# A fused recurrent-memory and spiking layer: norm statistics finished by GpSimd instead of VectorE, and ScalarE's queue reordered

## The chip, the cores and the metric

The kernel runs on one core of a Trainium2 chip. The metric is device time in microseconds (us), the median of several executions; lower is better. TensorE (PE in the profile; its weight loads are PEld), VectorE (DVE), ScalarE (ACT), GpSimd (POOL) and SyncE (SP) are processors with a queue each. Each works through its queue strictly in the order written, and they meet only through semaphores.

## The reference

The input is `x`, 8 batches of 512 tokens by 256 features. The layer is

```python
x = x + layernorm(attention(layernorm(x)))
x = x + layernorm(ffn(layernorm(x)))
```

with `layernorm(x) = (x - mean) / sqrt(var + 1e-5)` over the 256 features. `attention` projects to q, k and v (16 heads of 16), normalizes k inside each head, and runs a recurrence over the 512 tokens, `F = retention * F + coef * outer(v, k)`, `y = (W_LTM + F) q`, followed by an output projection. `ffn` is `relu(x W_fc)^2 W_proj`, followed by five spiking steps whose number of spikes, over 5, is its output. So every batch has four norms: norm 1 (input of attention), norm 2 (its output), norm 3 (input of the feed-forward part), norm 4 (the spike counts).

## The kernel before, in words

Everything is fp32 in on-chip memory. A batch is four tiles of 128 tokens (`TILES` = 4), or, with features first, two tiles of 128 features by 512 tokens.

**Slots.** The code is a software pipeline over batches. Function `run` calls `iteration(g, ...)` for g = 0 to 9 on every engine, and each iteration has 16 slots s. In iteration g the recurrence of batch g runs (flag `now`), while batch g+1 is prepared (`after`, b = g+1: norm 1, transposes, projections of k, q, v), batch g-1 goes through the output projection, norms 2 and 3 and the first feed-forward matmul (`before`, b1), and batch g-2 through the second feed-forward matmul, the spikes and norm 4 (`two_before`, b2). Iterations 2 to 6 have all four parts. Iteration 7 has no `after`, iteration 8 only `before` and `two_before`, iteration 9 only `two_before`. The slot and the place inside a slot fix the order of every engine's queue by hand; nothing else plans it.

**The recurrence.** In each slot VectorE makes two products (`hebbian`, L722) and two scans over 512 tokens (`scan`, L732). GpSimd multiplies the two states by q (`read`, L873, one 128x1024 operation per slot, done one slot later), and TensorE adds the products up every second slot (`sums`, L324). `read(g, 15)` stands in slot 0 of the next iteration, and `sums(g, 7)` in its slot 1. Reading needs the scans (`state_done`) and a free buffer of four (`sum_done`); the scans need a read buffer of four (`prod_done`).

**A norm.** VectorE's `statistics` makes `bn_stats` over four tiles (L679) and joins them with four `bn_aggr` (L686) into mean and variance. ScalarE's `deviation` takes the square root (L462). VectorE's `scales` takes the reciprocal (L692). ScalarE scales the four tiles (`norm`, L468; `norm4`, L474). Norms 1 to 3 subtract no mean (their inputs are centred through the weights); norm 4 does, through the offsets `nmr` = -mean/deviation, four small VectorE operations in `spike_offsets` (L697). GpSimd adds norm 4's result to the residual (`add_feed_forward`, L884, slot 13), and SyncE stores it.

**The keys.** `square_k` on ScalarE, `key_variance` on TensorE (L301), `key_deviation` on ScalarE (L497), `key_reciprocal` on VectorE (L709, `krd`), `spread_k`, `key_scale` on TensorE (L310), `norm_k` on VectorE (L714), and `copy_key` on ScalarE into PSUM (`p_k`), which the products read. This runs twice per batch: for half 1 in slots 1 to 8, for half 0 of the next batch in slots 11 to 16.

**The turn and the spikes.** In slots 6 and 7 TensorE transposes the normed input of the next batch into the bank `p_a` (`turn_x`, L275), and ScalarE copies each half out twice (`copy_xt`, L479: `xf`, then `xt`). The four parts of the second feed-forward matmul (`down`, L346) are copied by `copy_yf` (`yf`), five `signs` per pair of tiles follow (L547), and TensorE adds them up (`count_spikes`, L354). The count of the second pair waits for `signs(b2, 1)` in slot 8.

**ScalarE's queue before**, where the change touches it. Slot 0: `copy_key`, `deviation(1)`, `copy_v`, `hidden` 6 and 7. Slot 2: `copy_y`, `key_deviation`, `norm1`. Slot 3: two `copy_o`, `copy_q`. Slot 6: `copy_xt(b, 0)`, `copy_yf(b2, 2)`. Slot 7: `deviation(3)`. Slot 8: `copy_key`, `copy_xt(b, 1)`, `copy_yf(b2, 3)`, `norm` 3, `signs(b2, 1)`. Slot 11: `copy_y`, `deviation(4)`, `square_k`, `hidden` 1 and 2. Slot 12: `key_deviation`, `norm4`. Slot 13: `copy_q`, `spread_k`, `hidden` 3 and 4. Slot 15: `hidden` 5. A `hidden` is a Relu (L535, frees the bank for the up projection after next, L371) and a Square (L537).

Of the kernel before, what the change touches and what calls it, by code (L numbers as in the profile page):

```python
# [16 lines left out]
P = 128  # L17
# [51 lines left out]
def build(nc, x, w_qkv, w_o, w_fc, w_proj, w_ltm, head_params, shared_params, ident, head_mask, pick, out):  # L69
    ctx = ExitStack()  # L70
    with ctx:
# [6 lines left out]
        def sem(name):  # L78
# [34 lines left out]
        nmr = sb("nmr", [P, TILES])  # L113

# [42 lines left out]
            ones_ready wv_mean wv_centred wkq_mean wkq_centred wide_mean wide_copied wide_centred wo_mean wo_centred tables_done setup_step  # L157
# [6 lines left out]
            sign_done count_done spk_done n4_stats n4_var n4_dev n4_step n4_done res_done""".split()}  # L164
# [284 lines left out]
        def _(act):  # L449
# [9 lines left out]
            def deviation(n, b):  # L459
                act.wait_ge(S[f"n{n}_var"], at(b + 1))  # L460
                eps = eps_sb[:, 1:2] if n == 4 else eps_sb[:, 0:1]
                nc.scalar.activation(dev[n - 1][:, :], moments[n - 1][:, :, 1], ACT.Sqrt, bias=eps).then_inc(S[f"n{n}_dev"], 1)  # L462
# [8 lines left out]
            def norm4(b):  # L471
                act.wait_ge(S["n4_step"], at(2 * (b + 1)))
                for u in range(TILES):
                    nc.scalar.activation(spk[:, u, :], spk[:, u, :], ACT.Identity, scale=rdev[3][:, u:u + 1],  # L474
                                         bias=nmr[:, u:u + 1]).then_inc(S["n4_done"], 1)
# [110 lines left out]
            def iteration(g, now, before, two_before, after):  # L586
                b, b1, b2 = g + 1, g - 1, g - 2
                for s in range(SLOTS):
# [6 lines left out]
                    if s == 0:  # L595
                        if now and before: copy_key(g, 0)
                        if after: deviation(1, b)
                        if now: copy_v(g, 1)
                        if two_before:
                            hidden(b2, 6)  # L600
                            hidden(b2, 7)
                    if s == 1:
                        if now: square_k(g, 1)
                    if s == 2:
                        if before: copy_y(b1, 1)
                        if now: key_deviation(g, 1)
                        if after: norm1(b)
                    if s == 3:
                        if before:
                            copy_o(b1, 0)  # L610
                            copy_o(b1, 1)
                        if now: copy_q(g, 1)
                    if s == 4:
                        if before: deviation(2, b1)
                        if now: spread_k(g, 1)
                        if two_before: copy_yf(b2, 0)
# [49 lines left out]
        def _(dve):  # L666
# [8 lines left out]
            def statistics(n, b, src, ready, count):  # L675
# [6 lines left out]

                dve.wait_ge(S[f"n{n}_stats"], at(b + 1))
                dve.wait_ge(S[f"n{n}_step"], at(b if n < 4 else 2 * b))
# [52 lines left out]
            for j in range(STEPS):  # L737
                v.memset(drive_sb[:, j:j + 1], -DRIVES[j])
            v.memset(ones_sb[:, :], 1.0 / D).then_inc(S["ones_ready"], 1)
# [94 lines left out]
            def iteration(g, now, before, two_before, after):  # L834
                b, b1, b2 = g + 1, g - 1, g - 2
                for s in range(SLOTS):
# [10 lines left out]
                    if after and s == 2: scales(1, b)  # L847
                    if now and s == 4: key_reciprocal(g, 1)
                    if before and s == 4: statistics(2, b1, oo, "o_done", 2 * (b1 + 1))
                    if before and s == 5: scales(2, b1)  # L850
                    if now and s == 6: norm_k(g, 1)
                    if before and s == 7: statistics(3, b1, x1[b1 % 2], "x1_done", b1 + 1)
# [12 lines left out]
        def _(pool):  # L865
# [30 lines left out]

            low_x(0, 0)
# [13 lines left out]
            def iteration(g, now, before, two_before, after):  # L911
                b, b1, b2 = g + 1, g - 1, g - 2
                for s in range(SLOTS):
                    if s > 0 and now: read(g, s - 1)
# [8 lines left out]
                    if two_before and s == 13: add_feed_forward(b2)  # L923
# [53 lines left out]
```

## Time and profile before

| | |
|---|---|
| median of 3 runs | 638.61 us (637.57 to 639.96) |
| the profiled execution's own time | 633.62 us |
| its span, first to last instruction | 631.8 us |
| busy: VectorE / TensorE / GpSimd / ScalarE | 534.2 / 497.6 / 389.0 / 328.7 us |
| mean granted TensorE clock | 0.886 of full speed |

The span and the profiled execution's own time belong together; 1.8 us lie around the span. The median of the runs is 5.0 us above that execution. The first 35 us are setup, the recurrence runs from 35 us to 549 us, and the rest, some 83 us, finishes the last two batches without it. A busy share is an average over these stages. Which engine sets the pace in one of them has to be read from who waits for whom there.

### The profile page before, as it was taken

Reading aid. Unit: us, or ns where it says so; the run is one execution under the profiler, and the core shown is the slowest. Engines: PE = TensorE matmul, PEld = TensorE weight load, DVE = VectorE, ACT = ScalarE, POOL = GpSimd, SP = SyncE. Lnnn points to the kernel's source line nnn. Section 1 sums busy time; section 2 is a strip of 40 time slices with the busy share of each in tenths; the row PEclk is TensorE's granted clock in tenths of the full one; section 3 lists DMA queues with packets and bytes.
Section 4 is the critical chain, followed back from the end, with each engine's and each line's share of the span. In section 5 each row is a group of like instructions: output and inputs, shape, how many; then the busy total and the mean of one; then the engine's idle time right before and its main releaser. Section 6 shows DMA issues by size and latency. Waiting matters only on the chain.

```text
span 631.8 us, 7778 instructions
## 1 busy us (share of the span) xinstructions
PE 497.6 (79%) x2264; PEld 325.4 (52%) x2272; DVE 534.2 (85%) x933; ACT 328.7 (52%) x641; POOL 389.0 (62%) x186
## 2 busy tenths in 40 slices
PE   3585548359996999699969997899879996896891
PEld 1341225136673667365736575566646664484670
DVE  4799999997999999999999998999999999712001
ACT  4532113245647754675466636654666455636634
POOL 0048975785567766877687756875787677710201
PEclk9877667659997999899989989799979997978896
DMA  7475566456644774466556653577347844200000
GB/s 238 112 210 144 162 154 186 131 143 160 182 133 116 188 209 137 133 167 200 149 149 152 176 170 107 147 182 206 100 117 202 215 101 133 67 1 0 33 1 33
DMA packets 54730, 87.63 MB, mean 139 GB/s; under 512 B 5409, under 2 KB 19361, under 8 KB 54689
## 3 DMA queue, kind: packets, MB, share of 16 engines
q1 hardware_dynamic: 54112, 87.12, 49.9%
q8 instruction: 18, 0.29, 0.2%
q14 instruction: 24, 0.19, 0.1%
q10 hardware_dynamic: 576, 0.03, 0.1%
HBM read 78.74 MB, written 8.39 MB: 138 GB/s over the span
## 4 chain that ended last, share of the span: by engine, by line
PE 51%; issue 16%; DVE 15%; ACT 10%; POOL 6%; DMA 1%; POOLq 0%; ACTq 0%; DVEq 0%
PE p_c L346 13%; PE p_c L371 12%; DVE state L732 9%; PE p_a L281 6%; PE p_y L324 5%; PE p_c L337 4%; POOL prod L873 3%; ACT sign L547 3%; PE p_c L354 2%; PE p_a L301 2%; POOL x1t L889 2%; DVE p_u L722 2%; PE p_y L319 2%; ACT oo L468 1%; PE p_c L363 1%
## 5 line engine op out<-in xcount | busy, mean ns | idle before, releaser
L873 POOL TENSOR_TENSOR prod<-state,qf 128x1024 f32<-128x1024 f32 x128 | 303.1, 2373 | 140.4 <-DVE state L732 121.9
L732 DVE TENSOR_TENSOR_SCAN state<-ret,p_u 128x512 f32<-128x512 f32 x256 | 309.2, 1209 | 0.0
L722 DVE TENSOR_TENSOR p_u<-vrep,p_k 128x512 f32<-128x512 f32 x256 | 171.5, 676 | 2.5 <-ACT p_k L479 2.5
L346 PE MATMUL p_c<-wproj_sb,ht 128*128 128x256 f32 x512 | 116.1, 382 | 1.3 <-ACT ht L537 1.3
L346 PEld LDWEIGHTS p_c<-wproj_sb,ht 128*128 128x128 f32 x512 | 95.7, 190 | 24.3 <-issue 9.2
L371 PE MATMUL p_c<-x1t,wfc_s 128*128 128x512 f32 x384 | 98.9, 410 | 9.1 <-POOL x1t L889 8.0
L281 PE MATMUL p_a<-xt,wqkv_s 128*128 128x512 f32 x276 | 82.7, 438 | 10.6 <-POOL xt L889 3.0
L371 PEld LDWEIGHTS p_c<-x1t,wfc_s 128*128 128x128 f32 x384 | 73.9, 196 | 31.3 <-POOL x1t L889 12.3
L324 PE MATMUL p_y<-prod,summer 128*32 128x512 f32 x512 | 76.8, 675 | 10.4 <-POOL prod L873 10.4
L281 PEld LDWEIGHTS p_a<-xt,wqkv_s 128*128 128x128 f32 x276 | 53.3, 203 | 45.7 <-issue 16.9
L535 ACT ACTIVATE hr<-p_c 128x512 f32<-128x512 f32 x64 | 38.2, 597 | 34.6 <-PE p_c L371 32.6
L354 PE MATMUL p_c<-sign,ident_b 128*128 128x512 bf16 x72 | 24.2, 476 | 35.6 <-ACT sign L547 34.6
L547 ACT ACTIVATE sign<-yf,drive_sb 128x512 bf16<-128x512 f32 x80 | 50.6, 709 | 0.3
L679 DVE BATCH_NORM_STATS2 stats<-spk 128x6 f32<-128x256 f32 x32 | 11.1, 408 | 41.1 <-ACT spk L479 41.1
L884 POOL TENSOR_TENSOR x<-x,spk 128x1024 f32<-128x1024 f32 x8 | 19.2, 2398 | 42.2 <-ACT spk L474 42.2
L537 ACT ACTIVATE ht<-hr 128x512 f32<-128x512 f32 x64 | 40.4, 632 | 2.0
L462 ACT ACTIVATE dev<-moments,eps_sb 128x4 f32<-128x4 f32 x32 | 9.5, 297 | 53.5 <-DVE moments L686 53.5
L889 POOL TENSOR_TENSOR xt<-xf,xt 128x512 fp32r<-128x512 f32 x16 | 20.4, 1276 | 24.9 <-ACT xt L479 24.9
L337 PE MATMUL p_c<-wo_sb,yt 128*128 128x256 f32 x128 | 34.1, 426 | 0.8 <-ACT yt L479 0.8
L354 PEld LDWEIGHTS p_c<-sign,ident_b 128*128 128x128 bf16 x80 | 7.6, 109 | 51.8 <-ACT sign L547 38.5
L324 PEld LDWEIGHTS p_y<-prod,summer 128*32 128x32 f32 x512 | 10.6, 114 | 41.2 <-issue 24.1
L889 POOL TENSOR_TENSOR x1t<-x1f,x1t 128x512 fp32r<-128x512 f32 x16 | 20.1, 1280 | 17.5 <-ACT x1t L479 17.5
(107 smaller groups left out, 505.2 us busy)
## 6 DMA issues: line engine op xcount, KB each, us to landing
vrep<-v_rows SPq DMA_DIRECT2D x256, 256.0 KB, 3.6
xa<-in_x SPq DMA_DIRECT2D x8, 512.0 KB, 5.3
v_rows<-vf SPq DMA_DIRECT2D x16, 256.0 KB, 2.3
x<-in_x SPq DMA_DIRECT2D x8, 512.0 KB, 4.5
out<-x SPq DMA_DIRECT2D x8, 512.0 KB, 3.3
ht<-in_w_fc SPq DMA_DIRECT2D x1, 1024.0 KB, 7.6
wproj_sb<-in_w_proj SPq DMA_DIRECT2D x1, 1024.0 KB, 10.1
state<-in_w_qkv SPq DMA_DIRECT2D x1, 512.0 KB, 5.8
```

Source lines behind the costliest of these rows:

```text
L281: last = pe.matmul(bank[:, :], wqkv_s[:, i, t, first_col:first_col + P], xt[:, j, t, :], start=(t == i == j == 0), stop=(t == KT - 1 and i ...
L324: last = pe.matmul(p_y[32 * grp:32 * grp + 32, :], summer[:, half, dl, grp, :], prod[:, s % NZ, grp % 2, :], start=False, stop=(dl == 3), ...
L337: last = pe.matmul(p_c[(t + 1) % 2][:, i * D:(i + 1) * D], yt[:, half, tokens(2 * t + i)], wo_sb[:, half, :], start=(half == 0), stop=(hal ...
L346: last = pe.matmul(p_c[(u + 1) % 2][:, 0:D], ht[:, f, tokens(u)], wproj_sb[:, f, :], start=(f == 0), stop=(f == FT - 1))
L354: last = pe.matmul(p_c[(pair + 1) % 2][:, :], ident_b[:, :], sign[:, pair, j, :, :], start=(j == 0), stop=(j == STEPS - 1))
L371: last = pe.matmul(p_c[(f + 1) % 2][:, :], wfc_s[:, i, t, f * P:(f + 1) * P], x1t[:, j, t, :], start=(t == i == j == 0), stop=(t == KT - 1 ...
L537: nc.scalar.activation(ht[:, f, :], hr[:, f % 2, :], ACT.Square).then_inc(S["h_done"], 1)
L547: last = nc.scalar.activation(sign[:, pair, j, :, :], yf[:, 2 * pair:2 * pair + 2, :], ACT.Sign, bias=drive_sb[:, j:j + 1], scale=BELOW_ONE)
L722: v.tensor_tensor(p_u[n % NU][:, :], vrep[:, n % NV, :], p_k[:, :], ALU.mult).then_inc(S["hebb_done"], 1)
L732: v.tensor_tensor_scan(state[:, s % NS, i, :], ret[:, r:r + 1].broadcast_to([P, L]), p_u[n % NU][:, :], 0.0, ALU.mult, ALU.add).then_inc(S ...
L873: p.tensor_tensor(prod[:, s % NZ, :, :], state[:, s % NS, :, :], qf[:, s // HS, :].unsqueeze(1).broadcast_to([P, 2, L]), ALU.mult).then_in ...
L889: p.tensor_tensor(low, value, high.bitcast(F32), ALU.subtract).then_inc(S[done], 1)
```

## The change

- `statistics` on VectorE now only makes `bn_stats`. For norms 2 and 3 the `bn_aggr` follow as before (now `moments_of`). For norms 1 and 4 GpSimd joins the statistics: each `bn_stats` of 256 values leaves count, mean and sum of squares for its even and for its odd values, and GpSimd forms the sum of squares of all 256 as the sum of both plus (8 x difference of means)^2. These are five 128x4 `tensor_tensor` operations for norm 1 and six for norm 4 (it also needs the sum of the means), three of them followed by a wait for their own completion (`step`). ScalarE's square root takes `scale=1/D` with them.
- The spike offsets move from four VectorE operations to two GpSimd ones, with a `step` between.
- ScalarE's order: `deviation(1)` from slot 0 to slot 2, ahead of `copy_y`; `norm1` from slot 2 to the end of slot 3; `copy_xt(b, 0)` from slot 6 to slot 7, behind `deviation(3)`; `deviation(4)` behind `square_k` in slot 11; `norm4` from slot 12 to slot 14, behind `hidden` 3 and 4.
- VectorE: `scales(1)` from slot 2 to 3, `scales(4)` from slot 12 to 13, ahead of `key_reciprocal`.
- GpSimd: `moments_of(1)` at the head of slot 1, `moments_of(4)` at the head of slot 11, `spike_offsets` at the head of slot 14, `add_feed_forward` from slot 13 to slot 15, where it stands ahead of `read(g, 15)`.
- Two constant tiles are set on VectorE at the start. GpSimd waits for them, then makes `moments_of(1, 0)`.

```diff
@@ scalar @@
             def deviation(n, b):
                 act.wait_ge(S[f"n{n}_var"], at(b + 1))
-                eps = eps_sb[:, 1:2] if n == 4 else eps_sb[:, 0:1]
-                nc.scalar.activation(dev[n - 1][:, :], moments[n - 1][:, :, 1], ACT.Sqrt, bias=eps).then_inc(S[f"n{n}_dev"], 1)
+                if n in (1, 4):
+                    eps = eps_sb[:, 1:2] if n == 4 else eps_sb[:, 0:1]
+                    nc.scalar.activation(dev[n - 1][:, :], squares[n][:, :], ACT.Sqrt, bias=eps, scale=1.0 / D).then_inc(
+                        S[f"n{n}_dev"], 1)
...
             def norm4(b):
-                act.wait_ge(S["n4_step"], at(2 * (b + 1)))
+                act.wait_ge(S["n4_offset"], at(b + 1))
...
                     if s == 0:
                         if now and before: copy_key(g, 0)
-                        if after: deviation(1, b)
...
                     if s == 2:
+                        if after: deviation(1, b)
                         if before: copy_y(b1, 1)
                         if now: key_deviation(g, 1)
-                        if after: norm1(b)
                     if s == 3:
...
                         if now: copy_q(g, 1)
+                        if after: norm1(b)
...
                     if s == 6:
-                        if after: copy_xt(b, 0)
                         if two_before: copy_yf(b2, 2)
                     if s == 7:
                         if before: deviation(3, b1)
+                        if after: copy_xt(b, 0)
...
                         if now: copy_y(g, 0)
+                        if after: square_k(b, 0)
                         if two_before: deviation(4, b2)
-                        if after: square_k(b, 0)
...
                         if after: key_deviation(b, 0)
-                        if two_before: norm4(b2)
...
+                    if s == 14 and two_before: norm4(b2)
@@ vector @@
-            def spike_offsets(b):
-                dve.wait_ge(S["n4_step"], at(2 * b + 1))
-                for u in range(TILES):
-                    last = v.tensor_scalar(nmr[:, u:u + 1], moments[3][:, u, 0:1], rdev[3][:, u:u + 1], -1.0, ALU.mult,
-                                           ALU.mult)
-                last.then_inc(S["n4_step"], 1)
...
-                    if two_before and s == 12:
-                        scales(4, b2)
-                        spike_offsets(b2)
+                    if two_before and s == 13: scales(4, b2)
@@ gpsimd @@
+            def moments_of(n, b):
+                pool.wait_ge(S[f"n{n}_stats"], at(b + 1))
+                pool.wait_ge(S[f"n{n}_dev"], at(b))
+                means = [stats[n - 1][:, :, i] for i in (1, 4)]
+                sums = [stats[n - 1][:, :, i] for i in (2, 5)]
+                if n == 4:
+                    p.tensor_tensor(twice_mean[:, :], means[0], means[1], ALU.add)
+                p.tensor_tensor(squares[n][:, :], sums[0], sums[1], ALU.add)
+                step(p.tensor_tensor(spread[n][:, :], means[0], means[1], ALU.subtract))
+                step(p.tensor_tensor(spread[n][:, :], spread[n][:, :], eight[:, :], ALU.mult))
+                step(p.tensor_tensor(spread[n][:, :], spread[n][:, :], spread[n][:, :], ALU.mult))
+                p.tensor_tensor(squares[n][:, :], squares[n][:, :], spread[n][:, :], ALU.add).then_inc(S[f"n{n}_var"], 1)
+
+            def spike_offsets(b):
+                pool.wait_ge(S["n4_step"], at(b + 1))
+                pool.wait_ge(S["n4_done"], at(TILES * b))
+                step(p.tensor_tensor(twice_mean[:, :], twice_mean[:, :], minus_half[:, :], ALU.mult))
+                p.tensor_tensor(nmr[:, :], twice_mean[:, :], rdev[3][:, :], ALU.mult).then_inc(S["n4_offset"], 1)
...
                 for s in range(SLOTS):
+                    if after and s == 1: moments_of(1, b)
+                    if two_before and s == 11: moments_of(4, b2)
+                    if two_before and s == 14: spike_offsets(b2)
                     if s > 0 and now: read(g, s - 1)
...
-                    if two_before and s == 13: add_feed_forward(b2)
+                    if two_before and s == 15: add_feed_forward(b2)
```

## Rows read from the trace of the kernel before

**Rows 1.** The page's first part: busy us (share of the span) x instructions.

```profile
PE 497.6 (79%) x2264; PEld 325.4 (52%) x2272; DVE 534.2 (85%) x933; ACT 328.7 (52%) x641; POOL 389.0 (62%) x186
```

**Rows 2.** Timeline of VectorE: start us, us, engine, line, operation [idle before <-releaser].

```profile
276.55 0.58 DVE L697 TENSOR_SCALAR nmr<-moments,rdev 128x1 f32<-128x1 f32 x4
...
280.81 0.35 DVE L709 RECIPROCAL krd<-kdev 128x32 f32<-128x32 f32 x1 [0.25 <-ACT kdev L497]
...
289.62 1.38 DVE L679 BATCH_NORM_STATS2 stats<-xa 128x6 f32<-128x256 f32 x4
291.03 0.38 DVE L686 BATCH_NORM_AGGREGATE moments<-stats 128x2 f32<-128x6 f32 x4
...
321.61 0.38 DVE L686 BATCH_NORM_AGGREGATE moments<-stats 128x2 f32<-128x6 f32 x4
...
354.89 1.38 DVE L679 BATCH_NORM_STATS2 stats<-xa 128x6 f32<-128x256 f32 x4
...
421.82 1.38 DVE L679 BATCH_NORM_STATS2 stats<-xa 128x6 f32<-128x256 f32 x4
```

**Rows 3.** Who waited for whom: us in total, times, longest us.

```profile
PE p_y L324 <- POOL prod L873: 10.4, 4, 4.7
DVE krd L709 <- ACT kdev L497: 4.7, 6, 3.4
```

**Rows 4.** The chain that ended last, 288 to 352 us, its shares by line.

```profile
by line: PE p_c L346 22.2%; PE p_c L371 15.8%; PE p_a L281 9.4%; PE p_y L324 7.8%; PE p_c L337 5.6%; issue 5.3%; ACT sign L547 4.8%; POOL x1t L889 3.8%; PE p_c L354 3.6%; PE p_a L301 3.2%; PE p_y L319 2.7%; ACT oo L468 2.1%; ACT hr L535 1.9
```

**Rows 5.** Timeline of ScalarE in iterations 3 and 4.

```profile
288.25 0.60 ACT L535 ACTIVATE hr<-p_c 128x512 f32<-128x512 f32 x1 [1.71 <-PE p_c L371]
...
321.59 0.59 ACT L479 COPY xf<-p_a 128x512 f32<-128x512 f32 x1 [3.54 <-PE p_a L275]
...
322.73 0.37 ACT L479 COPY yf<-p_c 128x256 f32<-128x256 f32 x1
323.00 0.30 ACT L462 ACTIVATE dev<-moments,eps_sb 128x4 f32<-128x4 f32 x1
...
329.79 0.56 ACT L479 COPY spk<-p_c 128x512 f32<-128x512 f32 x1
```

**Rows 6.** Timeline of TensorE in iterations 4 and 7.

```profile
293.48 1.06 PE L324 MATMUL p_y<-prod,summer 128*32 128x512 f32 x8
...
297.56 1.06 PE L301 MATMUL p_a<-mean_sb,ksq 128*128 128x8 f32 x8 [1.44 <-ACT ksq L493]
...
329.94 2.31 PE L354 MATMUL p_c<-sign,ident_b 128*128 128x512 bf16 x5 [4.86 <-ACT sign L547]
...
524.25 1.46 PE L354 MATMUL p_c<-sign,ident_b 128*128 128x512 bf16 x5 [3.54 <-ACT sign L547]
```

**Rows 7.** Window: busy of PE, PEld, DVE, ACT, POOL; granted clock; DMA; GB/s.

```profile
330.00:332.00 2.00, 2.00 (x5) 0.74 (x6) 2.00 (x4) 0.35 (x1) 2.00 (x3) 0.50 0.94 243
```

**Rows 8.** GpSimd: timeline, then groups (busy, mean ns | idle before).

```profile
0.24 0.10 POOL L966 MEMSET const-float32-0.0<- 128x1 f32 x1 [0.24 <-issue]
...
285.19 7.11 POOL L873 TENSOR_TENSOR prod<-state,qf 128x1024 f32<-128x1024 f32 x3
...
L873 POOL TENSOR_TENSOR prod<-state,qf 128x1024 f32<-128x1024 f32 x128 | 303.1, 2373 | 140.4 <-DVE state L732 121.9 <-PE p_y L324 18.5
L889 POOL TENSOR_TENSOR x1t<-x1f,x1t 128x512 fp32r<-128x512 f32 x16 | 20.1, 1280 | 17.5 <-ACT x1t L479 17.5
```

**Rows 9.** Timelines of ScalarE, GpSimd and TensorE in the setup and the tail.

```profile
9.03 0.30 ACT L462 ACTIVATE dev<-moments,eps_sb 128x4 f32<-128x4 f32 x1 [0.20 <-DVE moments L686]
...
544.51 7.06 POOL L873 TENSOR_TENSOR prod<-state,qf 128x1024 f32<-128x1024 f32 x3
...
551.63 1.16 PE L324 MATMUL p_y<-prod,summer 128*32 128x512 f32 x8 [2.73 <-POOL prod L873]
...
595.50 4.37 PE L371 MATMUL p_c<-x1t,wfc_s 128*128 128x512 f32 x18 [1.15 <-ACT hr L535]
...
623.98 2.07 ACT L474 ACTIVATE spk<-spk,nmr,rdev 128x256 f32<-128x256 f32 x4 [0.86 <-DVE nmr L697]
```

More of the change, by code:

```diff
@@ L113, in build @@
         nmr = sb("nmr", [P, TILES])
+        squares = {n: sb(f"squares{n}", [P, TILES]) for n in (1, 4)}
+        spread = {n: sb(f"spread{n}", [P, TILES]) for n in (1, 4)}
+        twice_mean = sb("twice_mean", [P, TILES])
+        eight = sb("eight", [P, TILES])
+        minus_half = sb("minus_half", [P, TILES])
         xa = sb("xa", [P, TILES, D])
@@ L156, in build @@
             setup_ready setup_exp centred wv_high wv_low wk_high wk_low wq_high wq_low wide_high wide_low
-            ones_ready wv_mean wv_centred wkq_mean wkq_centred wide_mean wide_copied wide_centred wo_mean wo_centred tables_done setup_step
+            halves_set ones_ready wv_mean wv_centred wkq_mean wkq_centred wide_mean wide_copied wide_centred wo_mean wo_centred tables_done setup_step
             n1_stats n1_var n1_dev n1_step n1_done  xt_turned xt_done xt_high xt_low
@@ L163, in build @@
             up_done relu_done h_done down_done yf_done
-            sign_done count_done spk_done n4_stats n4_var n4_dev n4_step n4_done res_done""".split()}
+            sign_done count_done spk_done n4_stats n4_var n4_dev n4_step n4_offset n4_done pool_step res_done""".split()}
         v_in = [sem(f"v_in{i}") for i in range(NV)]
@@ L460, in deviation @@
                 act.wait_ge(S[f"n{n}_var"], at(b + 1))
-                eps = eps_sb[:, 1:2] if n == 4 else eps_sb[:, 0:1]
-                nc.scalar.activation(dev[n - 1][:, :], moments[n - 1][:, :, 1], ACT.Sqrt, bias=eps).then_inc(S[f"n{n}_dev"], 1)
+                if n in (1, 4):
+                    eps = eps_sb[:, 1:2] if n == 4 else eps_sb[:, 0:1]
+                    nc.scalar.activation(dev[n - 1][:, :], squares[n][:, :], ACT.Sqrt, bias=eps, scale=1.0 / D).then_inc(
+                        S[f"n{n}_dev"], 1)
+                else:
+                    nc.scalar.activation(dev[n - 1][:, :], moments[n - 1][:, :, 1], ACT.Sqrt, bias=eps_sb[:, 0:1]).then_inc(
+                        S[f"n{n}_dev"], 1)
             def norm(n, b, src, dst, used, count):
@@ L680, in statistics @@
                 last.then_inc(S[f"n{n}_stats"], 1)
+            def moments_of(n, b):
                 dve.wait_ge(S[f"n{n}_stats"], at(b + 1))
-                dve.wait_ge(S[f"n{n}_step"], at(b if n < 4 else 2 * b))
+                dve.wait_ge(S[f"n{n}_step"], at(b))
                 for u in range(TILES):
@@ L738, in _ @@
                 v.memset(drive_sb[:, j:j + 1], -DRIVES[j])
+            v.memset(eight[:, :], 8.0)
+            v.memset(minus_half[:, :], -0.5).then_inc(S["halves_set"], 1)
             v.memset(ones_sb[:, :], 1.0 / D).then_inc(S["ones_ready"], 1)
@@ L846, in iteration @@
                         scan(g, s, 0)
-                    if after and s == 2: scales(1, b)
+                    if after and s == 3: scales(1, b)
                     if now and s == 4: key_reciprocal(g, 1)
-                    if before and s == 4: statistics(2, b1, oo, "o_done", 2 * (b1 + 1))
+                    if before and s == 4:
+                        statistics(2, b1, oo, "o_done", 2 * (b1 + 1))
+                        moments_of(2, b1)
                     if before and s == 5: scales(2, b1)
                     if now and s == 6: norm_k(g, 1)
-                    if before and s == 7: statistics(3, b1, x1[b1 % 2], "x1_done", b1 + 1)
+                    if before and s == 7:
+                        statistics(3, b1, x1[b1 % 2], "x1_done", b1 + 1)
+                        moments_of(3, b1)
                     if two_before and s == 10: statistics(4, b2, spk, "spk_done", 2 * (b2 + 1))
-                    if two_before and s == 12:
-                        scales(4, b2)
-                        spike_offsets(b2)
+                    if two_before and s == 13: scales(4, b2)
                     if g == 0 and s == 13: mean_out()
@@ L895, in low_x1, with step, moments_of @@
                 rest(x1f[:, t, :], x1t[:, 0, t, :], x1t[:, 1, t, :], "x1t_high", KT * b + t + 1, "x1t_low")
+            steps = [0]
+            def step(ins):
+                steps[0] += 1
+                ins.then_inc(S["pool_step"], 1)
+                pool.wait_ge(S["pool_step"], steps[0])
+            def moments_of(n, b):
+                pool.wait_ge(S[f"n{n}_stats"], at(b + 1))
[14 more added lines that the diff above has]
+                p.tensor_tensor(nmr[:, :], twice_mean[:, :], rdev[3][:, :], ALU.mult).then_inc(S["n4_offset"], 1)
+            pool.wait_ge(S["halves_set"], 1)
+            moments_of(1, 0)
             low_x(0, 0)
```

## The prediction

> **What bounds the kernel now.** The page's busy shares come first and mislead: VectorE leads with 534.2 us [rows 1]. The timeline of VectorE gives the period: statistics of norm 1 start at 289.62, 354.89 and 421.82, so iteration 4 takes 65.27 us and iteration 5, 66.93 [rows 2]. VectorE fills nearly all of that, which looks like a bound. The waits say otherwise. VectorE stops for ScalarE's `kdev` (0.25 us at 280.81 [rows 2]; 6 times in all, one of 3.44 included [rows 3]), and that deviation follows TensorE's key variance. In the other direction TensorE's sums waited for GpSimd's products only 4 times [rows 3], in the first two iterations and the tail. The chain of waits through iteration 4 agrees: its thirteen largest entries are TensorE's, ScalarE's, issue time and one GpSimd operation that follows ScalarE; none is VectorE's [rows 4]. So in iterations 2 to 6 TensorE and ScalarE form a loop that paces itself, and VectorE has about 0.9 us spare in it. Iterations 0, 1 and 7 are paced by VectorE, setup and tail by the latency of a serial chain.
>
> The loop's one long hole is TensorE's wait of 4.86 us for the second pair of signs [rows 6]. Before them ScalarE works without a break from 321.59 (`xf`, released by TensorE) to 329.79 [rows 5], and TensorE then works at half clock until 334 us (0.50 in the window at 330 us [rows 7]).
>
> **The change part by part.** All terms are against the profiled execution's 633.62 us (span 631.8 and 1.8 around it). I carry the sum to the median, 5.0 us above, unchanged.
>
> *VectorE's removed work.* Four `bn_aggr` take 0.38 us and end as the next operation starts, about 0.40 from the queue [rows 2]. This goes twice per iteration. The offsets take 0.58, net 0.5 because the next operation overlaps [rows 2]. Together 1.3 us per full iteration. In iterations 2 to 6 it only lengthens the wait for `kdev`: worth 0 there, except for the phase below. In iterations 0 and 1 the queue is VectorE-bound up to that wait, and each loses one aggregate: **-0.8 us**.
>
> *GpSimd's price.* No small `tensor_tensor` is in the trace. A 128x1024 one costs 2373 ns, a 128x512 one 1280 [rows 8]. The line through both leaves 0.19 us at zero width. The ends are 0.10 (a one-column memset) and 1.28 (128x512) [rows 8]. I take 0.19, since four columns lie nearest to zero, and 0.25 for one followed by a step. `moments_of(1)` is then about 1.1 us, `moments_of(4)` 1.3, the offsets 0.5. The Trainium skill's GPSIMD Engine Reference (section 4.1) advises VectorE for elementwise work because GpSimd is about twice slower with two inputs. By that rule the move would lose; the sum below charges it only where the chain is serial.
>
> *Square roots in front.* In the block from 321.59, `yf` 2 and `dev` 3 stand at 322.73 and 323.00 behind `xf` and `xt` [rows 5]. Both come earlier now: `yf` 2 falls into the idle 3.54 us, and `dev` 3 goes as soon as its variance is there, 321.61 + 0.38 = 321.99 [rows 2]. VectorE reaches it 0.40 sooner (one aggregate less since `kdev`), so 321.6. It takes 0.2 of the queue, and `xf` starts at 321.83, 0.24 late. The block behind is shorter by 0.27 (`yf`) and 0.20 (`dev`). The spike count comes 0.23 us sooner. Five iterations (2 to 6): **-1.15 us**. `deviation(1)` in front of `copy_y` delays it 0.2, beside the key variance that starts at 297.56 [rows 6] and ends 0.9 later: 0. The waits of `norm1` and `deviation(4)` are covered by `copy_q` and `square_k`: 0.
>
> *`norm4` behind `hidden` 4.* Its 2.07 us [rows 9] go mostly into the 1.71 that `hidden` 5 waits for TensorE [rows 5]. `hidden` 5 comes some 0.3 late, and the bank it frees is needed just then: 0 to 0.1, taken as 0. Behind it `copy_key` is about 0.25 late, covered by statistics of norm 1 on VectorE, except in iteration 7, which has none.
>
> *`add_feed_forward` ahead of `read(g, 15)`.* Before, three reads ran without a gap from 285.19 to 292.30 [rows 8], the last one ending 1.2 us ahead of its sums at 293.48 [rows 6]. Now the addition of 2.4 us stands before the last one, while the others start up to 2.3 us earlier. Read 14 waits for its scan and ends at 288.7, `norm4` ends at 288.6, the addition at 291.1 and read 15 at 293.47. That is just when the sums want it: 0.05, taken as 0 per iteration. In iteration 7 nothing covers it. Reads ran from 544.51 to 551.57, and TensorE waits 2.73 us for the last [rows 9]. The addition puts 1.9 in front; VectorE's savings there (aggregate and offsets, 0.9, less 0.25 of `copy_key`) return 0.65: **+1.25 us**.
>
> *Setup and tail.* At the start, statistics to `dev` (9.03 [rows 9]) took 0.44 us. With GpSimd between it is 1.2, and VectorE's queue stands behind it: **+0.8**. In iteration 8 `norm4` moves from before `hidden` 3, where TensorE lost 1.15 [rows 9], to before `hidden` 5, where the last three hiddens queue behind it: **+0.3**. In iteration 9 all is serial. Moments cost 0.9 more than aggregates; offsets cost 0.5 against the 0.6 up to `norm4` at 623.98 [rows 9]: **+0.8**.
>
> Sum: -0.8 - 1.15 + 1.25 + 0.8 + 0.3 + 0.8 = **+1.2 us**. So 634.8 for such an execution and **639.8** for the median. At 1.28 us per small operation the serial places (5, 6 and 2 of them) add some 13 us; at 0.10 they give back 1.5.
>
> **The rivals.** *Slower: GpSimd's queue becomes late.* The place is read 15 behind the addition in slots 15 and 0. From the moment that read 15 ends over 0.3 us later than worked out (small operations of 0.6 us or more, or a late `norm4`), TensorE's sums, the key projection behind them and the loop lose it one for one. At 0.8 us in each of five iterations plus 2 more in setup and tail: 1.2 + 4 + 2, thus 645.8. For it speaks that the margin is nil at 293.47; against it that ScalarE is busy with `hidden` 7 then, which hides some 0.3, and that read 14 is timed by its scan. Chance 0.2.
>
> *Faster: TensorE's clock stays up.* The hole shrinks from 4.86 to about 4.4 us. The granted clock fell behind it in each of these iterations; at half clock the work from 329.94 to 334 costs about 2 us more than at full. If half the five falls are spared or shortened, -5: 634.8. Iteration 5 has a second fall behind the 1.44 us wait for `ksq`, which costs 66.93 - 65.27 = 1.7 [rows 2], and a shift of phase may remove or multiply it. The Trainium skill's TensorE: Matmul & The Clock Gate (section on HAM oscillation) says that idle gaps re-throttle the array and shorter ones keep it warm. By that rule any shortening could pay; the trace has a fall even behind a hole of 3.54 us, in iteration 7 [rows 6], which speaks against it. Chance 0.08.
>
> *Faster: VectorE is the bound after all.* If the loop follows VectorE's queue, 1.3 us in each of iterations 2 to 6 return: 6.5 less, 633.3. The nearly full queue speaks for it, the `kdev` waits against. Chance 0.1.
>
> *The change does nothing on the path* (no gain of 0.23, small costs as worked out): 641. It lies inside the forecast's own case.
>
> **How the numbers follow.** The forecast's case has 0.62 and spans 636 to 643: the price of small operations from 0.10 to 0.5, and one clock fall more or less (1.7). A measurement of this kernel can tell about 0.5%, 3.2 us, from no change: that is 635.4 to 641.8. Faster: 0.08 + 0.1, of which some ends inside: 0.16. Slower: 0.2 and the upper end of the forecast: 0.24. Same: 0.60. The range for 8 in 10 reaches down to 634 and up to 645.5.
>
> **What would show it.** Right: `bn_aggr` of norms 1 and 4 gone, VectorE busy down by some 10 us, its waits for `kdev` grown to about 1 us; the loop's period near 65.0; `dev` 3 ahead of `xf` and the hole at the signs near 4.4; the last read some 1.2 us later against its batch; small GpSimd operations near 0.2 us. Wrong: sums waiting for products in iterations 2 to 6, `kdev` waits unchanged with a period near 64, or small operations of 0.6 us and more.

## The result and the profile after

The changed kernel takes 640.74 us (median of 20 runs, 637.3 to 643.13), the kernel before 637.81 us (median of 20 runs beside them). The ratio is **1.0051**, 95% interval 1.0032 to 1.007: slower by about 3.2 us (interval 2.0 to 4.5), where 1.2 was forecast. The ratios here and below are those on record; they need not equal the quotient of two medians (2.9 us here). A second set of runs gave 1.003 (1.0005 to 1.0055), which has the forecast 1.2 us inside.

The page's busy line of the changed kernel, to be held against [rows 1]:

```profile
PE 502.4 (79%) x2272; PEld 328.1 (51%) x2272; DVE 521.8 (82%) x839; ACT 328.2 (51%) x641; POOL 407.8 (64%) x290
```

VectorE is relieved of 12.4 us, and the kernel is slower. The timeline of VectorE of the changed kernel (start us, us, operation [idle before <-releaser]) shows where the relief went:

```profile
37.43 1.40 DVE L689 BATCH_NORM_STATS2 stats<-xa 128x6 f32<-128x256 f32 x4
...
284.52 0.35 DVE L712 RECIPROCAL krd<-kdev 128x32 f32<-128x32 f32 x1 [1.37 <-ACT kdev L507]
...
293.33 1.38 DVE L689 BATCH_NORM_STATS2 stats<-xa 128x6 f32<-128x256 f32 x4
...
358.45 1.38 DVE L689 BATCH_NORM_STATS2 stats<-xa 128x6 f32<-128x256 f32 x4
...
425.02 1.38 DVE L689 BATCH_NORM_STATS2 stats<-xa 128x6 f32<-128x256 f32 x4
```

It waits 1.37 us for the key deviation (the `krd` row) where it waited 0.25 [rows 2]. Iteration 4 takes 65.12 us instead of 65.27 (iterations 2 and 3: 65.10 and 65.09), and iteration 5, 66.57 instead of 66.93. The recurrence opens at 37.43 us, read from the statistics that VectorE makes in its first slot. In the trace of before the same statistics stood at 32.38.

ScalarE's timeline shows the block ahead of the second signs, to be held against [rows 5]: deviation 3 comes first, `yf` 2 has gone into the idle time ahead.

```profile
321.27 0.35 ACT L489 COPY yf<-p_c 128x256 f32<-128x256 f32 x1
325.34 0.30 ACT L471 ACTIVATE dev<-moments,eps_sb 128x4 f32<-128x4 f32 x1 [3.71 <-DVE moments L696]
325.54 0.57 ACT L489 COPY xf<-p_a 128x512 f32<-128x512 f32 x1
...
333.25 0.57 ACT L489 COPY spk<-p_c 128x512 f32<-128x512 f32 x1
```

TensorE's timeline shows the turn, the second spike count, and in the tail the wait for the last product [rows 6, 9]:

```profile
324.76 0.60 PE L280 MATMUL p_a<-ident_sb,xa 128*128 128x128 f32 x4
...
333.40 2.32 PE L359 MATMUL p_c<-sign,ident_b 128*128 128x512 bf16 x5 [4.38 <-ACT sign L557]
...
555.43 1.94 PE L329 MATMUL p_y<-prod,summer 128*32 128x512 f32 x8 [4.78 <-POOL prod L880]
```

The hole is 4.38 us (4.86 before), and turn to count is 8.64 us. Before it was 9.04, from the turn below to the count at 329.94 [rows 6]:

```profile
320.90 0.60 PE L275 MATMUL p_a<-ident_sb,xa 128*128 128x128 f32 x4
```

GpSimd's timeline has the small operations in the setup, read 15 behind the addition where iteration 3 goes over into 4, and the same in the tail:

```profile
9.07 0.20 POOL L920 TENSOR_TENSOR squares<-stats 128x4 f32<-128x4 f32 x1 [8.63 <-DVE stats L689]
9.23 0.20 POOL L921 TENSOR_TENSOR spread<-stats 128x4 f32<-128x4 f32 x1
9.51 0.20 POOL L922 TENSOR_TENSOR spread<-spread,eight 128x4 f32<-128x4 f32 x1
...
290.19 2.41 POOL L880 TENSOR_TENSOR prod<-state,qf 128x1024 f32<-128x1024 f32 x1 [1.12 <-PE p_y L329]
292.56 2.40 POOL L891 TENSOR_TENSOR x<-x,spk 128x1024 f32<-128x1024 f32 x1
294.92 2.39 POOL L880 TENSOR_TENSOR prod<-state,qf 128x1024 f32<-128x1024 f32 x1
...
550.73 2.35 POOL L891 TENSOR_TENSOR x<-x,spk 128x1024 f32<-128x1024 f32 x1
553.03 2.35 POOL L880 TENSOR_TENSOR prod<-state,qf 128x1024 f32<-128x1024 f32 x1
```

The two profiled executions differ by 637.4 - 631.8 = 5.6 us, the medians by 2.9. The profiled execution of before took 633.62 us, 4.2 below its kernel's median; that of the changed kernel took 639.36, 1.4 below. So some 2.8 us of the differences in the table below come from which executions were profiled:

| stretch | before | changed | difference |
|---|---|---|---|
| start to statistics of norm 1, batch 1 | 32.38 | 37.43 | +5.05 |
| to the same of batch 7 (six iterations) | 389.44 | 387.59 | -1.85 |
| to the last scan's end | 127.32 | 126.12 | -1.20 |
| to the statistics of norm 2 in iteration 8 | 11.68 | 13.99 | +2.31 |
| to the last norm's statistics | 60.15 | 60.52 | +0.37 |
| to the end | 10.83 | 11.75 | +0.92 |

The setup is the one stretch far from the forecast, so the experiments start with it.

### The profile page after: what moved, and what is told of

It is laid out like the page before. It is cut to its first block, busy times and chain, and to the rows that moved or that the text cites. A ratio compares the mean times of both kernels' runs of the same rounds, so it can differ in the third digit from the quotient of the medians.

```text
span 637.4 us, 7804 instructions
## 1 busy us (share of the span) xinstructions
PE 502.4 (79%) x2272; PEld 328.1 (51%) x2272; DVE 521.8 (82%) x839; ACT 328.2 (51%) x641; POOL 407.8 (64%) x290
## 4 chain that ended last, share of the span: by engine, by line
DVE 33%; PE 29%; issue 21%; ACT 10%; POOL 4%; DMA 1%; POOLq 0%; DVEq 0%; ACTq 0%
DVE state L735 20%; PE p_c L376 7%; PE p_c L351 7%; DVE p_u L725 6%; DVE stats L689 4%; ACT sign L557 3%; PE p_a L286 3%; PE p_y L329 3%; PE p_c L359 2%; POOL x1t L896 2%; PE p_c L342 2%; POOL prod L880 2%; PE p_a L306 1%; ACT oo L478 1%; PE p_c L368 1%
## 5 line engine op out<-in xcount | busy, mean ns | idle before, releaser
L286 PE MATMUL p_a<-xt,wqkv_s 128*128 128x512 f32 x276 | 85.0, 447 | 11.6 <-POOL xt L896 4.4
L376 PEld LDWEIGHTS p_c<-x1t,wfc_s 128*128 128x128 f32 x384 | 72.5, 193 | 33.3 <-POOL x1t L896 13.3
L329 PE MATMUL p_y<-prod,summer 128*32 128x512 f32 x512 | 74.9, 660 | 12.7 <-POOL prod L880 12.7
L359 PE MATMUL p_c<-sign,ident_b 128*128 128x512 bf16 x80 | 27.2, 485 | 32.3 <-ACT sign L557 32.3
L342 PE MATMUL p_c<-wo_sb,yt 128*128 128x256 f32 x128 | 36.3, 447 | 0.9 <-ACT yt L489 0.9
L489 ACT COPY vf<-p_a 128x512 f32<-128x512 f32 x15 | 8.8, 586 | 47.3 <-PE p_a L286 47.3
L342 PEld LDWEIGHTS p_c<-wo_sb,yt 128*128 128x128 f32 x128 | 28.5, 229 | 7.4 <-issue 2.6
```

Of the source, the lines that this page charges most:

```text
L286: last = pe.matmul(bank[:, :], wqkv_s[:, i, t, first_col:first_col + P], xt[:, j, t, :], start=(t == i == j == 0), stop=(t == KT - 1 and i ...
L329: last = pe.matmul(p_y[32 * grp:32 * grp + 32, :], summer[:, half, dl, grp, :], prod[:, s % NZ, grp % 2, :], start=False, stop=(dl == 3), ...
L342: last = pe.matmul(p_c[(t + 1) % 2][:, i * D:(i + 1) * D], yt[:, half, tokens(2 * t + i)], wo_sb[:, half, :], start=(half == 0), stop=(hal ...
L359: last = pe.matmul(p_c[(pair + 1) % 2][:, :], ident_b[:, :], sign[:, pair, j, :, :], start=(j == 0), stop=(j == STEPS - 1))
L376: last = pe.matmul(p_c[(f + 1) % 2][:, :], wfc_s[:, i, t, f * P:(f + 1) * P], x1t[:, j, t, :], start=(t == i == j == 0), stop=(t == KT - 1 ...
```

## The experiments

Medians below are of runs taken beside runs of the kernel before. The kernel before itself had 639.58, 638.55 and 636.76 us in the three sets, so ratios are to be compared inside a set. In every full iteration TensorE's granted clock falls once near the spike count; "quiet" means an iteration without an additional fall.

**The changed kernel again.** No edit.

> The changed kernel once more, as the partner of the runs beside it. My theory: slower than the kernel before by 1.2 us of serial work plus whatever the setup adds, so a ratio of 1.002 to 1.006; the period of iterations 2 to 4 is 65.10 us again. The question it serves: the changed kernel's one trace opens the recurrence 5.05 us later than the trace of before (37.43 against 32.38 us), of which only 0.9 is GpSimd's chain. If TensorE's half clock in the setup is a matter of the execution, this trace may show another opening, nearer 33.5 us; if it follows from the change, it shows 37 us again.

Measured: 640.45 us against 639.58, ratio 1.003 (1.0005 to 1.0055). The recurrence opened at 33.23 us in this trace, 4.2 us before the other one of the same kernel:

```profile
33.23 1.39 DVE L689 BATCH_NORM_STATS2 stats<-xa 128x6 f32<-128x256 f32 x4
```

That is 0.85 us behind the 32.38 of before, about GpSimd's chain: its square root starts 1.35 us after the statistics end (8.94 to 10.29 in the first trace), where it was 0.44. TensorE's timeline tells the two executions apart. The key projection of the setup, first in the trace of the result, then in this one:

```profile
25.73 2.93 PE L286 MATMUL p_a<-xt,wqkv_s 128*128 128x512 f32 x6 [1.07 <-DVE wqkv_s L805]
```

```profile
25.33 1.66 PE L286 MATMUL p_a<-xt,wqkv_s 128*128 128x512 f32 x6 [1.52 <-DVE wqkv_s L805]
```

The same six matmuls take 2.93 us at half clock and 1.66 at full. So most of the 5.05 us was the clock of one execution. Nor did it last. Here iterations 0, 1 and 2 took 61.09, 67.24 and 66.67 us where the first trace had 59.85, 65.85 and 65.10. At the start of iteration 3 the two executions stand at 228.23 and 228.24 us: nothing is left of the 4.2 us.

**Norm 1 of batch 0 on VectorE.**

```diff
-                if n in (1, 4):
+                if n in (1, 4) and not (n == 1 and isinstance(b, int) and b == 0):
...
             statistics(1, 0, xa, "x_in", 16)
+            moments_of(1, 0)
...
             pool.wait_ge(S["halves_set"], 1)
-            moments_of(1, 0)
```

> Norm 1 of batch 0 has its moments from VectorE's bn_aggr again, all else as changed. Theory A (the setup's loss is the 0.9 us of the serial GpSimd chain and the rest is chance of the clock): 0.9 us less than the changed kernel, reciprocal about 0.45 us after the deviation starts as before. Rival B (the late start pushes TensorE's setup work into the half clock each time): 3 to 5 us less than the changed kernel, and the recurrence opens near 32.5 us.

Measured: 639.82 us, ratio 1.0021 (0.9996 to 1.0045), 0.6 us under the changed kernel beside it, inside the noise. The opening was at 33.94 us. The size fits A and speaks against a loss of 3 to 5 us in each run, but it does not settle a smaller tendency. Over all thirteen traces of this study the seven with GpSimd in the setup opened at 33.2, 35.5, 37.0, 37.1, 37.2, 37.4 and 37.8 us (mean 36.5). The six without opened at 32.4, 33.6, 33.9, 34.5, 36.1 and 36.3 (mean 34.5). The means are 2.0 us apart, 0.9 of it the chain. The start follows the clock: the mean granted clock from 20 to 32 us is 0.68 to 0.86 in the six traces that open by 35.5 us, and 0.51 to 0.64 in the five later ones that have a record there. Whether GpSimd's chain makes the half clock more likely stays open. By the start of iteration 3 little of it is left. In the eleven traces with the changed order that start lies at 228.4 us on average with GpSimd in the setup (seven, 226.6 to 230.9) and at 227.7 without (four, 225.3 to 229.0).

**The addition of iteration 7 behind read 15.**

```diff
-                    if two_before and s == 15: add_feed_forward(b2)
+                    if two_before and s == 15 and g != B - 1: add_feed_forward(b2)
...
                     if s == 0 and before: read(b1, SLOTS - 1)
+                    if s == 0 and g == B: add_feed_forward(b2 - 1)
```

> Only in iteration 7 the feed-forward addition goes behind read 15 (in iteration 8's slot 0). Theory A (in the tail nothing covers the addition): read 15 starts 2.3 us earlier against the last scan, TensorE's wait for it falls from 4.78 to about 2.5 us, and the kernel takes 2.3 us less than the changed one. Rival B (the read is not what the tail waits for): no change.

Measured: 637.89 us, ratio 0.9984 (0.9957 to 1.001), 2.6 us under the changed kernel of the same set (640.45). TensorE's wait for read 15 falls from 4.78 to 2.96 us (2.5 expected):

```profile
552.20 1.93 PE L329 MATMUL p_y<-prod,summer 128*32 128x512 f32 x8 [2.96 <-POOL prod L880]
```

From the last scan to the statistics of norm 2 it is 11.41 us (13.99 and 13.54 in the two traces of the changed kernel). In this trace the next stretch took 62.05 us (60.52 and 60.65), so that 0.7 to 1.1 us of the gain reached the end; the 2.6 us are the medians', and the intervals of the two ratios overlap a little. Theory A holds: one queue position, in one of ten iterations, is the largest single loss of the change that a run shows.

**The last norm's moments and offsets on VectorE.** `moments_of(4, b2)` and four `tensor_scalar` stand in VectorE's slots 10 and 13 when b2 is the last batch, and GpSimd skips them then:

```diff
-                    if two_before and s == 13: scales(4, b2)
+                    if two_before and s == 10 and b2 == B - 1: moments_of(4, b2)
+                    if two_before and s == 13:
+                        scales(4, b2)
+                        if b2 == B - 1: spike_offsets(b2)
```

> The changed kernel with only the last batch's norm 4 (moments and offsets) on VectorE. Theory A: from the last statistics to the end 10.8 us as in the kernel before, not 11.75; 0.9 us less in all, which a measurement hardly tells. Rival B (the tail hides it): 11.75 us again.

Measured: 640.17 us, ratio 1.0042 (1.001 to 1.0075). The last stretch is 10.81 us (10.83 before, 11.75 changed): the 0.9 us are there in the trace, and the runs can't tell them, as expected.

**All serial places at once.** The three edits above, and `norm4` of batch 6 behind `hidden` 7:

```diff
-                    if s == 14 and two_before: norm4(b2)
+                    if s == 14 and two_before and g != B: norm4(b2)
...
                             hidden(b2, 7)
+                            if g == B + 1: norm4(b2 - 1)
```

> All serial places put right at once, the loop left as changed: batch 0's norm 1 and the last batch's norm 4 (moments and offsets) on VectorE, the addition of iteration 7 behind read 15, and norm4 of batch 6 behind hidden 7. Theory A: 0.9 + 2.3 + 1.0 + 1.1 = 5.3 us less than the changed kernel, about 2 us (0.3%) faster than the kernel before, a ratio near 0.997. Rival B (the loss sits in the steady iterations): ratio stays above 1.003.

Measured: 636.08 us against 639.58, ratio 0.9957 (0.9924 to 0.999). This beats the changed kernel of the same set by 4.4 us, near the 5.3 of theory A. The loss does not sit in the steady iterations. A second set tests its gain over the kernel before:

> The kernel with all serial places put right, once more with five rounds, to settle whether it beats both. It was 0.9957 of the kernel before, interval 0.9924 to 0.999. Theory A: the ratio stays between 0.993 and 0.999. Rival B (that was the luck of its rounds): 1.000 or more.

Measured: 635.18 us against 636.76, ratio 1.0003 (0.9976 to 1.0029). That is what rival B says: the gain over the kernel before did not repeat. The version no longer shows the change's loss in either set. In this one the kernel with only the last norm undone had 1.0042, and the one without the GpSimd part (below) 1.0043. That it beats the kernel before is not shown.

**Is VectorE the bound?** Idle work on it, twelve `bn_aggr` that nobody uses:

```diff
+                    if two_before and after and s == 12:
+                        for u in range(3 * TILES):
+                            v.bn_aggr(pad[:, u, :], stats[3][:, u % TILES, :])
                     if two_before and s == 13: scales(4, b2)
```

> The changed kernel with 12 idle bn_aggr (about 1.2 us) added on VectorE in slot 12 of iterations 2 to 6, whose result nobody uses. Theory A (TensorE and ScalarE pace these iterations, VectorE waits 1.37 us there for the key deviation): the wait shrinks to about 0.2 us and the period stays 65.1 us. Rival B (VectorE paces them): the period grows by 1.2 us, the time by 6 us.

Measured: 641.86 us, ratio 1.0059 (1.0027 to 1.0091). VectorE's timeline has the idle work, the wait, and the statistics that open iteration 4:

```profile
283.84 0.88 DVE L866 BATCH_NORM_AGGREGATE pad<-stats 128x2 f32<-128x6 f32 x12
...
288.65 0.35 DVE L713 RECIPROCAL krd<-kdev 128x32 f32<-128x32 f32 x1 [0.44 <-ACT kdev L508]
...
297.45 1.38 DVE L690 BATCH_NORM_STATS2 stats<-xa 128x6 f32<-128x256 f32 x4
```

The twelve took 0.88 us, not 1.2. The wait fell by about that, from 1.37 to 0.44 us, and iterations 4 and 5 took 64.93 and 65.36 us (iterations 2 and 3, with an additional clock fall each, 66.68 and 66.53). The rival asks for 0.9 us in each of five iterations. The ratio lies only 0.5 to 1.9 us above the changed kernel's two, and no quiet iteration grew by it: VectorE does not pace the changed kernel's steady iterations.

**GpSimd's margin.** One idle 128x512 operation ahead of read 15 in iterations 2 to 6:

```diff
+                    if s == 0 and before and two_before and after: p.tensor_tensor(pad[:, :], pad[:, :], pad[:, :], ALU.mult)
                     if s == 0 and before: read(b1, SLOTS - 1)
```

> The changed kernel with one idle 128x512 operation (1.28 us) on GpSimd ahead of read 15 in slot 0 of iterations 2 to 6. Theory A (read 15 ends exactly when TensorE's sums want it, and ScalarE's hidden 7 covers about 0.3 us more): TensorE's sums wait 1.2 us for the product and the period grows by 0.9 to 1.0 us, the time by 4 to 5 us. Rival B (GpSimd has room there): period unchanged.

Measured: 646.95 us (four runs), ratio 1.0134 (1.0083 to 1.0185), by the ratios 5.3 to 6.6 us above the changed kernel of the other sets, where 4 to 5 were expected. GpSimd's and TensorE's timelines:

```profile
362.82 1.05 POOL L959 TENSOR_TENSOR pad<-pad 128x512 f32<-128x512 f32 x1
...
366.26 1.06 PE L330 MATMUL p_y<-prod,summer 128*32 128x512 f32 x8 [0.96 <-POOL prod L882]
```

The idle operation took 1.05 us, the sums waited 0.96, and quiet iteration 4 took 65.81 us, 0.7 more (0.9 to 1.0 expected). Iterations 3 and 5 took 67.70 and 67.51 with an additional clock fall each; iteration 2, whose sums did not wait, kept 65.13. So the margin is about 0.1 us for TensorE's wait, and 0.25 more did not reach the period. The slow rival's mechanism is real. Small operations of 0.20 us just did not reach it.

**The swap alone, on the kernel before.**

```diff
                     if s == 6:
-                        if after: copy_xt(b, 0)
                         if two_before: copy_yf(b2, 2)
                     if s == 7:
                         if before: deviation(3, b1)
+                        if after: copy_xt(b, 0)
```

> The kernel before, with only the first half of the turned input's copies moved behind deviation 3. Theory A (the deviation takes its place only when VectorE delivers the variance, 0.4 us later here than in the changed kernel): the copy starts 0.64 us late, the block behind is 0.47 shorter, the period of iterations 2 to 4 grows from 65.27 to about 65.4 us; the time is the same within noise. Rival B (square roots in front are a gain by themselves): the period falls to 65.0 or less.

Measured: 636.65 us, ratio 0.9978 (0.9937 to 1.0019). The turn-to-count distance grew as theory A has it, 9.37 us against 9.04:

```profile
321.65 0.60 PE L275 MATMUL p_a<-ident_sb,xa 128*128 128x128 f32 x4
...
331.02 1.72 PE L354 MATMUL p_c<-sign,ident_b 128*128 128x512 bf16 x5 [4.41 <-ACT sign L547]
```

Iteration 2 took the expected 65.4 us (160.04 to 225.48). Yet iterations 3, 4 and 5 took 65.05, 65.06 and 65.06, less than in the kernel before. The windows around the count of iteration 4 (busy us (x) of PE, PEld, DVE, ACT, POOL, granted clock, DMA, GB/s) show why, first the kernel before, then this one:

```profile
328.00:330.00 2.00, 0.06 (x1) 0.07 (x2) 2.00 (x4) 2.00 (x5) 1.88 (x1) 0.50 0.95 279
...
334.00:336.00 2.00, 2.00 (x13) 0.94 (x13) 1.97 (x8) 1.54 (x3) 1.50 (x3) 1.00 0.00 0
```

```profile
328.00:330.00 2.00, 0.00 (x0) 0.00 (x0) 2.00 (x3) 2.00 (x4) 0.84 (x2) 1.00 0.98 246
330.00:332.00 2.00, 0.98 (x4) 0.46 (x5) 2.00 (x3) 1.43 (x3) 2.00 (x2) 0.92 1.09 329
332.00:334.00 2.00, 2.00 (x8) 1.35 (x7) 2.00 (x3) 0.90 (x2) 2.00 (x2) 0.50 0.44 102
334.00:336.00 2.00, 2.00 (x13) 0.65 (x12) 1.97 (x10) 1.94 (x4) 2.00 (x2) 0.73 0.00 0
```

Before, the clock fell in the hole and half clock lasted until 334 us, 4 us past the count at 329.94. Here it fell only after the count, near 332, and was back at 335, some 3.4 us of half clock on work. Iteration 2 of this same trace is the counter-check. There the clock was down before the count at 200.53, the half clock on work lasted 4.8 us, and the period was the expected 65.44:

```profile
200.00:202.00 2.00, 1.47 (x4) 0.58 (x5) 2.00 (x4) 0.94 (x2) 2.00 (x2) 0.50 1.09 300
```

So a distance 0.33 us longer was paid back where the fall was shorter. In these VectorE no longer waits for the key deviation at all (0.25 us before), only 0.91 us for a copied key: with the moments still on VectorE, its queue has no other wait left to give.

**The swap undone, on the changed kernel.** The reverse of the diff above.

> The changed kernel with only the turned input's first copies back in slot 6, ahead of deviation 3. Theory A (the block of ScalarE ahead of the second signs is 0.4 us shorter in the changed kernel, and the half clock behind it gives part of that back or takes it): the distance from TensorE's turn to the second spike count goes from 8.64 back to about 9.04 us, the hole from 4.38 to about 4.86. The period of a quiet iteration rises by 0.2 to 0.4 us if the half clock begins before the count as in the changed kernel, and less or not at all if it begins elsewhere. Time within 0.3% of the changed kernel. Rival B (the swap is worth nothing or a loss): distance and period unchanged.

Measured: 644.1 us (six runs), ratio 1.0123 (1.0089 to 1.0158). The changed kernel was not run in this set; its nearest relative there, with only the last norm's moments undone, has 640.17, 3.9 us or 0.6% less. The expected "within 0.3%" was missed. The hole is back at 4.85 us and turn to count at 9.04. Quiet iterations take 65.45 to 65.50 us, 0.38 more than in the changed kernel:

```profile
259.31 0.60 PE L280 MATMUL p_a<-ident_sb,xa 128*128 128x128 f32 x4
...
268.35 2.32 PE L359 MATMUL p_c<-sign,ident_b 128*128 128x512 bf16 x5 [4.85 <-ACT sign L557]
```

Rival B falls. Five such iterations are 1.9 us. In the one trace the rest came with clock falls (iteration 4 took 67.17 us, and 67.25 lie between the counts of iterations 5 and 6) and an opening at 37.84. Why all six runs are above 642.5 us stays open.

**The change without its GpSimd part.** The changed order, with `bn_aggr` and the offsets on VectorE for all four norms:

```diff
-                if n in (1, 4):
+                if False:
...
-                    if two_before and s == 13: scales(4, b2)
+                    if two_before and s == 13:
+                        scales(4, b2)
+                        spike_offsets(b2)
...
-                    if after and s == 1: moments_of(1, b)
-                    if two_before and s == 11: moments_of(4, b2)
-                    if two_before and s == 14: spike_offsets(b2)
```

> The changed kernel's order on all engines, with moments and offsets back on VectorE: the change without its GpSimd part. Theory A (VectorE's 1.3 us per iteration only lengthen its wait for the key deviation): quiet iterations take 65.0 to 65.2 us, as in the changed kernel, and VectorE's wait for the key deviation falls from 1.37 to about 0.1 us; the setup saves 0.9, the last norm 0.9, and the first two iterations and iteration 7 lose 1.7 together, so the time is that of the changed kernel within noise. Rival B (VectorE paces the loop): quiet iterations of 66 us or more, the time 5 us or more above the changed kernel.

Measured: 639.38 us, ratio 1.0043 (1.0016 to 1.007), between the changed kernel's 1.0051 and 1.003 of other sets, as A has it. The wait for the key deviation is 0.17 to 0.45 us. But quiet iterations take 65.49 to 65.52 us, not 65.1. ScalarE's and TensorE's timelines:

```profile
260.35 0.30 ACT L472 ACTIVATE dev<-moments,eps_sb 128x4 f32<-128x4 f32 x1 [3.72 <-DVE moments L697]
260.55 0.56 ACT L490 COPY xf<-p_a 128x512 f32<-128x512 f32 x1
```

```profile
259.36 0.60 PE L280 MATMUL p_a<-ident_sb,xa 128*128 128x128 f32 x4
...
268.41 2.31 PE L359 MATMUL p_c<-sign,ident_b 128*128 128x512 bf16 x5 [4.38 <-ACT sign L558]
```

The deviation starts 0.99 us after the turn, in the changed kernel 0.58 (325.34 - 324.76). In the changed kernel, with `bn_aggr` of norm 1 (0.40 us) gone from its queue, VectorE reaches the variance of norm 3 that much sooner, and ScalarE's block waits for it. Turn to count is 9.05 us against 8.64. So GpSimd's part is worth 0.4 us per steady iteration, by this one phase, and spends it again elsewhere: 0.9 us each in the setup and the last norm are shown.

## Why the prediction was right, and where it was off

- **The number** is nearer than the working. The median was forecast at 639.8 us and came at 640.74. The sum, though, was made for the profiled execution, 634.8 us, and the changed kernel's took 639.36. The 5.0 us from execution to median, carried unchanged, were 1.4 for the changed kernel and, over 20 runs, 4.2 for the kernel before, whose median came 0.8 below the 638.61 taken. That the two gaps met is in part luck. As a difference, 1.2 us were forecast, below the interval of the first set (2.0 to 4.5) and inside that of the second (0.3 to 3.5).
- **The bound** was read rightly. Relief of VectorE went into its wait (0.25 to 1.37 us), and 0.88 us of idle work went back into it without a trace in the quiet periods.
- **GpSimd's price** was right: 0.20 us measured, 0.28 from one stepped operation to the next, for 0.19 and 0.25 taken by the line through two wide operations. The fear that the move loses because GpSimd is slower (the Trainium skill, GPSIMD Engine Reference, section 4.1) was borne out only where the chain is serial.
- **Square roots in front**: turn to count fell by 0.40 us where I had 0.23, mostly because `xf` starts only 0.09 us later behind the turn (0.78 against 0.69), not 0.24. The period fell only by 0.17 (65.27 to 65.10). Followed along TensorE's timeline from the count of iteration 3, 0.23 us were given back: 0.09 in the work behind the count, 0.12 by the time of the sums at 294.74, around `hidden` 5 and the bank it frees, which I had put at 0, and 0.05 up to the sums that read 15 feeds, less 0.03 behind them. The sizes were off, not the mechanism.
- **Read 15**: the margin was seen. It ended at 297.31 us, 0.06 ahead of its sums at 297.37. The working was off in one point: read 14 waited for TensorE (1.12 us), not for its scan. In the tail the two traces have +2.31 and +1.86 us, where I had 1.9. The -1.20 us over iterations 6 and 7 can't be set against it: the second trace of the changed kernel took 128.24 us there, more than the 127.32 of before.
- **Iterations 0 and 1** were forecast 0.8 us shorter. Iteration 0 was 61.1 us in most traces of the changed order (61.53 before), the aggregate's 0.4. Iteration 1 is not paced by VectorE, as I had it: VectorE waits there 3.44 us for the key deviation before [rows 3], and 3.51 and 4.90 in the two traces of the changed kernel, with the clock. Its length ranges from 63.5 to 67.3 us over all traces.
- **Iteration 8** cost 0.37 (0.3 forecast) and **the last norm** 0.92 (0.8).
- **The setup term** treated TensorE's clock as unchanged. The serial part was 0.85 us for the 0.8 taken, but the opening moves by 5 us with the clock, from 32.4 to 37.8 us over thirteen traces.
- **The missing 2 us** (3.2 measured, 1.2 forecast) are not located. The setup is a poor place for them: of the 2.0 us between the groups' openings, 0.7 is left by iteration 3. The serial places together are worth 4.4 us by the medians, where the terms behind them had 3.8, and the steady gain was 0.06 us per iteration short. The rest lies within what clock falls move from one execution to the next.
- **The rivals**: GpSimd late is real as a mechanism, shown by the added operation, but did not decide. The fast clock rival did not come: holes of 4.38 us had a fall behind or in them each time, so "any shortening could pay" did not hold. The swap alone shows that a fall can be shortened by timing. VectorE as the bound was excluded for the changed kernel.

## What to carry to other kernels

A queue with 98% busy time (VectorE before: 64.19 of the 65.27 us of iteration 4) can still be off the path: look for its waits on the others, and for theirs on it, before paying for its relief. When work goes to an engine with slack, price three places apart: the steady loop, the serial setup, and the tail, where a queue position that was free in the loop (an addition ahead of the last read) costs most of its length (1.9 to 2.3 of 2.35 us). Undo such a move only where the chain is serial. And before stages of two traces are compared, hold each profiled execution against its kernel's median: here one lay 4.2 us below it and the other 1.4, which is as much as the effect.

## What was not expected of the hardware

- The granted clock in the windows is 1.00 from 8 to 40 us in the changed kernel, although the matmuls of that stretch show the half clock (2.93 us for six against 1.66). Where the record has no entry yet, the matmul's duration is the better witness.

```profile
24.00:32.00 8.00, 5.76 (x17) 3.99 (x16) 5.79 (x26) 3.45 (x7) 0.00 (x0) 1.00 0.41 121
```

- A fall of TensorE's clock is not placed by the wait alone. In iteration 4, behind holes of 4.86 (before), 4.38 (changed) and 4.41 us (swap alone), work at half clock lasted 4.1, 4.6 and 3.4 us, so a shorter hole did not shorten it. Nor does its length alone set the period: in the kernel before it was 4.9, 4.5 and 4.1 us in iterations 2, 3 and 4, which took 65.28, 65.25 and 65.27. And of two holes of 3.54 us in iteration 7, the one before had a fall behind it, at 525.16 us, and the one of the swap alone had none until 533.
- A 128x512 product of a tile with itself took 1.05 us on GpSimd, a difference of two tiles, written as fp32r, 1.28 [rows 8]. Which of the differences between them counts was not tried.
